# Causal attention: products and values moved around the score pairs of a step on TensorE

## The chip, the cores and the metric

The kernel runs on one NeuronCore of a Trainium2 chip. The engines that matter here are TensorE (PE; its weight loads are listed as PEld), VectorE (DVE) and ScalarE (ACT); each works through an instruction stream of its own, and semaphores tie them together. The metric is the time of one execution on the device in microseconds (us), the median of the runs.

## The reference, cut to what matters

A network of four layers, each with an attention and a feed-forward part, on 1024 tokens of 256 features, in float32. Two of its attentions are causal, with 16 heads of width 16, on one sequence of all 1024 tokens. The first is:

```python
_d['L0_attn_x'] = jax.random.normal(..., (1, 1024, 256), dtype=_x0.dtype)

def _L0_attn_ref(x, Wq, bq, Wk, bk, Wv, bv, Wo, bo):
    b, s, _ = x.shape                     # 1, 1024
    q = rope(proj(Wq, bq)); k = rope(proj(Wk, bk)); v = proj(Wv, bv)
    attn = jnp.einsum('bhqd,bhkd->bhqk', q, k) * scale
    causal = jnp.triu(jnp.ones((s, s), dtype=bool), k=1)
    attn = jnp.where(causal, -jnp.inf, attn)
    attn_weights = jax.nn.softmax(attn, axis=-1)
    out = jnp.einsum('bhqk,bhkd->bqhd', attn_weights, v)
    return jnp.einsum('bse,fe->bsf', out.transpose(0, 2, 1, 3).reshape(b, s, E), Wo) + bo
```

The other, in the feed-forward part of the second layer (`_attention` in `_L1_ffn_ref`), computes the same without rope and biases. Everything else of the network is untouched.

## The kernel before

The stages run one after another; `attend_causal` (L1114) is the body of both causal attentions, with the prefix a0h in the first and a2h in the second. It is cut into eight units: a unit is four heads (a quad Q) and one half of the queries (h, 512 of them), in the order (Q0,h0), (Q1,h0), (Q0,h1), (Q1,h1), then the same for Q2 and Q3.

The exponentials need the maximum of each row beforehand, so two kinds of work go on at once, some units apart:

- 48 **steps** g (4 of a unit with h=0, 8 with h=1), one for each block of 128 keys. A step has two **score pairs**, `scores(g, 0)` and `scores(g, 1)` (L1355), here S0 and S1: two heads each, keys by up to 512 queries, into three PSUM banks in turn. ScalarE takes four exponentials of them (L1455). **V**, `values(g - 1)` (L1377), multiplies the four results of the step in front with the values. 32 of the steps are diagonal: their scores get mask products (L1285) and are 512, 384, 256, 128 wide in turn.
- 48 **visits** x, one for each block of 128 queries and 512 keys. A visit, here A, has products in two pairs (L1313), each into one of two PSUM pairs, and VectorE takes the row maxima of them (L1481). For 32 of the visits, the diagonal ones, masks (L1285, eight products) come behind both pairs. Visit g+9 stands in step g from step 7 on; the first steps have two visits, and the last, 38, is that of visit 47. Steps 39 to 47 have none.

Single **events** on TensorE stand between them: **M** (L1338, the maxima of a unit turned into a row, which VectorE adds to the queries, L1497; steps 3, 7, 15, 19, 23, 31, 39), **P** (L1296 and L1297, eight times a quad's queries or keys put in place, which ScalarE copies, L1440 and L1442; steps 12, 13, 14 twice, 16, 17, 18 twice), **D** (L1388, the denominators of a unit, read by VectorE, L1504; steps 6, 10, 18, 26, 30, 34, 42 and one behind the last) and **R** (L1397, their reciprocals back, which VectorE multiplies with the unit's sums, L1512; steps 8, 12, 20, 28, 32, 36, 44 and one behind the last).

A's two pairs and all events share the two PSUM pairs in turn, `spare(key)`, by a count over all of them; `wait_spare` makes each wait until what lay there two uses before was read (`a_read`, `m_added`, `rounded`, `r_steps`, `on_done`). The first step of a unit waits for its M to be added (`m_added`). S0 of a step waits for the third exponential of the step in front, S1 for the first of its own, V for the last of the step in front (`p_ready`).

In a step of the loop at the end of TensorE's stream stand S0, A (with its masks; in step 39 M), S1, a second visit, M or P, V, then D and R. The order of all events on ScalarE and VectorE is fixed by the same table `after`.

Of the kernel before, what the change touches and what calls it, by code (L numbers as in the profile page):

```python
# [1113 lines left out]
def attend_causal(nc, core, name, qk, v, scale, masks_dram, before, sync, gpsimd):  # L1114
# [33 lines left out]
    for Q in range(2, QUADS):  # L1148
        x = min(x for x, vi in enumerate(visits) if UNITS[vi[0]][0] == Q)
# [19 lines left out]
    with ExitStack() as ctx:  # L1169
# [94 lines left out]
        def seg(x):  # L1264

            w, qb, s = visits[x]
            diag = s == UNITS[w][1]
            return qb, s, ((qb + 1) * P - s * HALF if diag else HALF), diag
# [12 lines left out]
        def _(pe):  # L1281
# [19 lines left out]
            def maxima(x):  # L1301

                w = visits[x][0]
                Q, h = UNITS[w]
                qb, s, n, diag = seg(x)
                if h == 0 and qb == 0:
                    pe.wait_ge(rounded, 4 * (Q + 1))
                for p in range(2):
                    wait_spare(pe, ("A", x, p))
                    ps = spare(("A", x, p))  # L1310
                    for u in range(2):
                        rows = slice(64 * u, 64 * u + K)
                        mm = pe.matmul(ps[:, u, 0:n], qt[rows, 2 * (Q % SLOTS) + p, qb * P:(qb + 1) * P],  # L1313
                                       kt[rows, 2 * (Q % SLOTS) + p, s * HALF:s * HALF + n], start=True, stop=not diag,
                                       tile_position=(64 * u, 0))
                    if not diag:
                        mm.then_inc(a_ready, 1)
                    elif x < 4:
                        mask_pair(x, p, n)
                if diag and x >= 4:  # L1320
                    for p in range(2):
                        mask_pair(x, p, n)

# [18 lines left out]
            def scores(g, p):  # L1342

                w, kb = steps[g]
                Q, h = UNITS[w]
                c0, n, diag = width(g)
                if kb == 0 and p == 0:
                    pe.wait_ge(m_added, w + 1)
                    pe.wait_ge(rounded, len(FIRST))
                if 4 * g + 2 * p >= 2:  # L1350
                    pe.wait_ge(p_ready, 4 * g + 2 * p - 1)
                for u in range(2):
                    t = 4 * g + 2 * p + u
                    rows = slice(64 * u, 64 * u + K)
                    mm = pe.matmul(core.bank[2 + t % 3][:, 0:n], kt[rows, 2 * (Q % SLOTS) + p, kb * P:(kb + 1) * P],  # L1355
                                   qt[rows, 2 * (Q % SLOTS) + p, h * HALF + c0:(h + 1) * HALF], start=True,
                                   stop=not diag, tile_position=(64 * u, 0))
                    if not diag:
                        mm.then_inc(s_ready, 1)
                if diag:  # L1360
                    for c in range(2):
                        for u in range(2):
                            t = 4 * g + 2 * p + u
                            mm = mask(pe, core.bank[2 + t % 3][:, 64 * c:64 * c + 64], 1, c, u)
                            if c == 1:
                                mm.then_inc(s_ready, 1)

            def values(g):

                w, kb = steps[g]  # L1370
                Q, h = UNITS[w]
                c0, n, diag = width(g)
                if kb == 0 and w:
                    pe.wait_ge(ou_done, w)
                pe.wait_ge(p_ready, 4 * g + 4)
                for b in range(4):
                    mm = pe.matmul(core.bank[5][32 * b:32 * b + 32, c0:HALF], v[:, kb, 4 * Q + b, :],  # L1377
                                   prob[:, (4 * g + b) % NP, 0:n], start=kb == 0, stop=kb == KEYS_OF[h] - 1,
                                   skip_group_check=True, tile_position=(0, 32 * b))
                mm.then_inc(av_done, 1)  # L1380
# [20 lines left out]
            def others(events):  # L1401
                for kind, x, *c in events:
                    if kind == "A":
                        maxima(x)
                    elif kind == "M":
                        max_rows(x)
                    elif kind == "D":
                        sums(x)
                    elif kind == "P":
                        place(x, c[0])  # L1410
                    else:
                        inverse(x)

            others(head)
            for g in range(len(steps) + 6):
                events = [e for e in after[g] if e[0] in "APM"]
                if g < len(steps):
                    scores(g, 0)
                    others(events[:1])
                    scores(g, 1)  # L1420
                    events = events[1:]
                others(events)
                if 0 < g <= len(steps):
                    values(g - 1)
                others([e for e in after[g] if e[0] in "DR"])

# [2120 lines left out]
```

## Time and profile before

| | us |
|---|---|
| median of 3 runs | 2784.68 (2775.67 to 2786.64) |
| the profiled execution | 2789.25 |
| its span | 2787.5 |
| first causal attention's steps (a0h), from the span's start | 68.4 to 249.9 |
| second one's (a2h) | 1469.9 to 1656.7 |

Of the span TensorE is busy for 2531.3 us, VectorE for 1627.8, ScalarE for 1259.5, GpSimd for 1289.6. In a timeline a row is one instruction or several alike that follow each other: start, length, engine, line of the code, operation, what it writes and reads, and in brackets how long the engine had been idle and what ended that. PEclk is the granted clock of TensorE as a share of full speed. A step's start is the start of its first L1355 row.

### The profile page before, as it was taken

What the parts mean: (1) busy time and instruction counts of PE and PEld (TensorE: products, weight loads), DVE (VectorE), ACT (ScalarE), POOL (GpSimd) and SP (SyncE); (2) the same over time, 40 slices, a digit from 0 to 9 for tenths busy, and PEclk for the clock granted to TensorE, in tenths of its full rate; (3) what the DMA queues carried; (4) which work ended last, traced back from release to release, by engine and by line L of the source; (5) the groups of instructions that cost most, each with busy time, mean ns of one, the idle gap of its engine ahead of it and who ended that gap; (6) DMA issues with size and microseconds to landing.
All of it is one profiled execution on the core that took longest, in us unless ns stands there. A gap on an engine that the chain in (4) does not pass through costs nothing. (4 is left out here: it accounts for less than half of the span.)

```text
span 2787.5 us, 40697 instructions
## 1 busy us (share of the span) xinstructions
PE 2531.3 (91%) x14471; PEld 1686.6 (61%) x14474; DVE 1627.8 (58%) x2168; ACT 1259.5 (45%) x2174; POOL 1289.6 (46%) x1130
## 2 busy tenths in 40 slices
PE   6887999878999999999878888789999989998798
PEld 4444777654444444444664446578888867776676
DVE  4663555577666766664436633477767745554555
ACT  4464333464555555555334552256555543333222
POOL 4100344486888888888521003254545523442243
PEclk9798999898999999999976979899999998998799
DMA  1000111121101101010000001100100001110111
GB/s 58 1 2 15 35 46 48 44 79 38 39 16 38 39 24 38 16 35 1 27 24 1 1 1 49 52 22 20 31 20 20 21 10 41 45 45 15 30 42 41
DMA packets 39709, 81.63 MB, mean 29 GB/s; under 512 B 7552, under 2 KB 21120, under 8 KB 39040
## 3 DMA queue, kind: packets, MB, share of 16 engines
q1 hardware_dynamic: 39264, 79.41, 10.2%
q8 instruction: 98, 1.61, 0.3%
q14 instruction: 59, 0.48, 0.1%
q10 hardware_dynamic: 288, 0.13, 0.0%
HBM read 59.07 MB, written 2.62 MB: 22 GB/s over the span
## 5 line engine op out<-in xcount | busy, mean ns | idle before, releaser
L2017 DVE TENSOR_REDUCE a1h_mseg<-bank 128x2 f32<-128x1024 f32 x256 | 302.7, 1222 | 187.3 <-PE bank L1774 173.4
L63 POOL TENSOR_TENSOR f_wh<-f_raw,ones_r 128x768 fp32r<-128x768 f32 (+1 forms) x74 | 111.8, 1511 | 545.6 <-PE bank L464 367.2
L1951 ACT ACTIVATE a1h_prob<-bank 128x512 f32<-128x512 f32 x366 | 206.1, 598 | 165.8 <-PE bank L1834 83.8
L1754 POOL TENSOR_TENSOR a_qk<-a_qk,a1h_prob 128x512 f32<-128x512 f32 x186 | 238.7, 1315 | 50.8 <-ACT a1h_prob L1951 50.8
L453 PE MATMUL bank<-x_norm_h,f_wh 128*128 128x512 f32 x592 | 244.2, 412 | 6.5 <-PEq L3247 2.5
L453 PE MATMUL bank<-x_norm_l,f_wh 128*128 128x512 f32 x592 | 238.7, 403 | 0.0
L453 PE MATMUL bank<-x_norm_h,f_wl 128*128 128x512 f32 x592 | 237.5, 401 | 0.0
L656 DVE SCALAR_TENSOR_TENSOR f_tf<-bank,f_bias,f_sg 128x512 f32<-128x512 f32 x148 | 111.0, 751 | 191.8 <-PE bank L453 185.4
L1832 PE MATMUL bank<-a1h_ql,a1h_k 128*128 128x512 f32 x512 | 203.2, 397 | 0.0
L544 ACT ACTIVATE f_hhi<-f_hf 128x512 fp32r<-128x512 f32 x124 | 78.3, 632 | 276.3 <-DVE f_hf L664 276.3
L1847 PE MATMUL bank<-a1h_prob,a_v 128*64 128x512 f32 x732 | 179.8, 604 | 0.0
L670 DVE TENSOR_TENSOR f_hlo<-f_hf,f_hhi 128x512 fp32r<-128x512 f32 x124 | 116.1, 938 | 82.7 <-ACT f_hhi L544 82.4
L533 ACT ACTIVATE f_sg<-bank,f_bias 128x512 f32<-128x512 f32 x148 | 101.9, 688 | 130.1 <-PE bank L453 130.1
L453 PEld LDWEIGHTS bank<-x_norm_h,f_wh 128*128 128x128 f32 x592 | 114.0, 192 | 50.8 <-issue 24.3
L453 PEld LDWEIGHTS bank<-x_norm_l,f_wh 128*128 128x128 f32 x592 | 114.1, 193 | 28.2
L364 POOL TENSOR_TENSOR f_wl<-f_raw,f_wh 128x768 fp32r<-128x768 f32 (+1 forms) x74 | 127.8, 1727 | 5.9
L453 PEld LDWEIGHTS bank<-x_norm_h,f_wl 128*128 128x128 f32 x592 | 114.7, 194 | 25.5
L464 PE MATMUL bank<-f_hhi,f_wh 128*128 128x512 f32 x296 | 118.5, 400 | 12.8 <-DVE f_hlo L670 12.8
L1831 PE MATMUL bank<-x_norm_h,a1h_kn 128*128 128x512 f32 x256 | 120.4, 470 | 4.7 <-DVE a1h_k L2012 3.4
L2871 POOL TENSOR_TENSOR l2a_rope<-l2a_rope,l2a_tab 128x512 f32<-128x512 f32 x64 | 81.2, 1276 | 88.9 <-ACT l2a_rope L2736 87.8
L1754 POOL TENSOR_TENSOR x_norm<-x_norm,a1h_prob 128x512 f32<-128x512 f32 x86 | 112.3, 1338 | 20.6 <-ACT a1h_prob L1951 20.6
L1455 ACT ACTIVATE a2h_prob<-bank 128x512 f32<-128x512 f32 (+3 forms) x192 | 83.7, 488 | 81.2 <-PE bank L1285 56.9
(595 smaller groups left out, 6337.8 us busy)
## 6 DMA issues: line engine op xcount, KB each, us to landing
f_raw<-in_l_w_dram SPq DMA_DIRECT2D x66, 385.0 KB, 3.1
a1h_st_q<-a_qk SPq DMA_DIRECT2D x128, 128.0 KB, 2.4
l2a_qkraw<-in_l2a_wqk_dram SPq DMA_DIRECT2D x32, 128.0 KB, 2.1
l2a_vraw<-in_l2a_wvg_dram SPq DMA_DIRECT2D x8, 512.0 KB, 3.8
f_raw<-in_l_w_dram SPq DMA_DIRECT2D x8, 449.0 KB, 3.3
a_qk<-l_keys SPq DMA_DIRECT2D x24, 128.0 KB, 2.8
a1p_raw<-in_l1a_w_dram SPq DMA_DIRECT2D x20, 128.0 KB, 2.1
a_qk<-in_l1a_wo_dram SPq DMA_DIRECT2D x16, 128.0 KB, 2.1
```

The lines of the kernel that those rows point to most:

```text
L63: return pool.tensor_tensor(dst, src, one.to_broadcast(list(src.shape)), ALU.mult)
L364: pool.tensor_tensor(wl[:, slot, :], raw[:, slot, 0:B], wh[:, slot, :].bitcast(F32), ALU.subtract).then_inc(w_split, 1)
L453: mm = pe.matmul(out[:, :], w[:, slot, c0:c0 + P], x, start=n == 0, stop=n == 3 * n_k - 1)
L464: mm = pe.matmul(acc[m][h][:, :], w[:, slot, c0:c0 + P], x[:, h, :], start=begin and n == 0, stop=False, skip_group_check=True)
L656: dve.scalar_tensor_tensor(tf[:, h, :], up[h][:, :], bias[:, slot, 1:2], sg[:, h, :], ALU.add, ALU.mult).then_inc(t_ready, 1)
L670: dve.tensor_tensor(hl[:, h, :], src[:, h, :], hh[:, h, :].bitcast(F32), ALU.subtract).then_inc(hl_ready, 1)
L1754: pool.tensor_tensor(out, first, slot_of[t % NP], ALU.add).then_inc(sum_done, 1)
L1831: pe.matmul(bank[:, :], kn[:, G % 2, a, keys], QA[n % 2][:, a, half(h)], start=True, stop=False)
L1832: mm = pe.matmul(bank[:, :], k1[:, a, keys], ql[:, n % 2, a, half(h)], start=False, stop=lo >= hi)
L1847: pe.matmul(core.bank[5][64 * a:64 * a + 64, :], v[:, kb, 2 * (n // 4) + a, :], slot_of[t % NP], start=kb == 0, stop=kb == TB - 1, skip_gr ...
L1951: act.activation(slot_of[t % NP], core.bank[2 + t % 3][:, :], ACT.Exp, scale=scale).then_inc(p_ready, 1)
L2017: dve.tensor_reduce(mseg[:, :, qb, s], spare(("A", n, k))[:, :, :], AX.X, ALU.max).then_inc(a_read, 1)
```

## The change

For a step with a visit TensorE's stream is now: both pairs of A, S0, the masks of A, V, S1, then a second visit with its masks, M or P, D and R. A step without a visit has S0, its M if there is one (step 39), V, S1, D and R. In the first step there is no V in front; that of the last step stands alone behind it. The head of the stage, and the streams of the other engines, are as before, and so is the turn in which A and the events use the two PSUM pairs.

```diff
--- before.py
+++ after.py
@@ -1317,7 +1317,11 @@
                         mm.then_inc(a_ready, 1)
                     elif x < 4:
                         mask_pair(x, p, n)
-                if diag and x >= 4:
+
+            def mask_maxima(x):
+
+                qb, s, n, diag = seg(x)
+                if diag:
                     for p in range(2):
                         mask_pair(x, p, n)
 
@@ -1402,6 +1406,8 @@
                 for kind, x, *c in events:
                     if kind == "A":
                         maxima(x)
+                        if x >= 4:
+                            mask_maxima(x)
                     elif kind == "M":
                         max_rows(x)
                     elif kind == "D":
@@ -1415,12 +1421,20 @@
             for g in range(len(steps) + 6):
                 events = [e for e in after[g] if e[0] in "APM"]
                 if g < len(steps):
+                    visit = events[0][1] if events and events[0][0] == "A" else None
+                    if visit is not None:
+                        maxima(visit)
                     scores(g, 0)
-                    others(events[:1])
+                    if visit is None:
+                        others(events[:1])
+                    else:
+                        mask_maxima(visit)
+                    if g:
+                        values(g - 1)
                     scores(g, 1)
                     events = events[1:]
                 others(events)
-                if 0 < g <= len(steps):
+                if g == len(steps):
                     values(g - 1)
                 others([e for e in after[g] if e[0] in "DR"])
```

TensorE in step 16, first attention, and at the start of step 17, before (names: put is the matrix that places a quad, P's products; prob the exponentials):

```order
L1355 MATMUL bank<-a0h_qt,a0h_kt 128x512 [waits a0h_p_ready]
L1355 MATMUL bank<-a0h_qt,a0h_kt 128x512
L1296 MATMUL bank<-x_norm_h,a0h_put 128x512 [waits a0h_lo1,a0h_a_read]
L1297 MATMUL bank<-x_norm_l,a0h_put 128x512
L1296 MATMUL bank<-x_norm_h,a0h_put 128x512
L1297 MATMUL bank<-x_norm_l,a0h_put 128x512
L1377 MATMUL bank<-a0h_prob,a_v 32x128 [waits a0h_p_ready]
L1377 MATMUL bank<-a0h_prob,a_v 32x128 x3
L1355 MATMUL bank<-a0h_qt,a0h_kt 128x512 [waits a0h_p_ready]
L1355 MATMUL bank<-a0h_qt,a0h_kt 128x512
L1313 MATMUL bank<-a0h_kt,a0h_qt 128x384 [waits a0h_a_read]
L1313 MATMUL bank<-a0h_kt,a0h_qt 128x384
```

And now, where L1359 and L1381 are the old L1355 and L1377:

```order
L1359 MATMUL bank<-a0h_qt,a0h_kt 128x512 [waits a0h_p_ready]
L1359 MATMUL bank<-a0h_qt,a0h_kt 128x512
L1296 MATMUL bank<-x_norm_h,a0h_put 128x512 [waits a0h_lo1,a0h_a_read]
L1297 MATMUL bank<-x_norm_l,a0h_put 128x512
L1296 MATMUL bank<-x_norm_h,a0h_put 128x512
L1297 MATMUL bank<-x_norm_l,a0h_put 128x512
L1313 MATMUL bank<-a0h_kt,a0h_qt 128x384 [waits a0h_a_read]
L1313 MATMUL bank<-a0h_kt,a0h_qt 128x384
L1313 MATMUL bank<-a0h_kt,a0h_qt 128x384 [waits a0h_rounded]
L1313 MATMUL bank<-a0h_kt,a0h_qt 128x384
L1359 MATMUL bank<-a0h_qt,a0h_kt 128x512 [waits a0h_p_ready]
L1359 MATMUL bank<-a0h_qt,a0h_kt 128x512
```

V (L1377) has left its place behind P and stands between S0 and S1 of its step; the next visit, whose second pair waits for ScalarE's copy of P (`rounded`), stands in front of the next S0 instead of behind it.

TensorE around R, from S1 of step 20 to S0 of step 21, before:

```order
L1355 MATMUL bank<-a0h_qt,a0h_kt 128x512 [waits a0h_p_ready]
L1355 MATMUL bank<-a0h_qt,a0h_kt 128x512
L1285 MATMUL bank<-a0h_mk 128x64 x4
L1377 MATMUL bank<-a0h_prob,a_v 32x512 [waits a0h_p_ready]
L1377 MATMUL bank<-a0h_prob,a_v 32x512 x3
L1397 MATMUL bank<-ident,a0h_rx 128x128 [waits a0h_rx,a0h_a_read]
L1397 MATMUL bank<-ident,a0h_rx 128x128 x3
L1355 MATMUL bank<-a0h_qt,a0h_kt 128x384 [waits a0h_p_ready]
```

And now (L1401 is the old L1397):

```order
L1359 MATMUL bank<-a0h_qt,a0h_kt 128x512 [waits a0h_p_ready]
L1359 MATMUL bank<-a0h_qt,a0h_kt 128x512
L1285 MATMUL bank<-a0h_mk 128x64 x4
L1401 MATMUL bank<-ident,a0h_rx 128x128 [waits a0h_rx,a0h_a_read]
L1401 MATMUL bank<-ident,a0h_rx 128x128 x3
L1313 MATMUL bank<-a0h_kt,a0h_qt 128x384 [waits a0h_a_read]
L1313 MATMUL bank<-a0h_kt,a0h_qt 128x384
L1313 MATMUL bank<-a0h_kt,a0h_qt 128x384 [waits a0h_on]
L1313 MATMUL bank<-a0h_kt,a0h_qt 128x384
L1359 MATMUL bank<-a0h_qt,a0h_kt 128x384 [waits a0h_p_ready]
```

R follows S1 directly, and the visit with its wait for VectorE's multiply (`on`) lies between R and the next S0.

## Rows read from the trace of the kernel before

**Rows 1.** Stretches of both attentions: length, busy us (instructions) by engine, PEclk, DMA.
```profile
core 0: us, PE busy (x) PEld busy (x) DVE busy (x) ACT busy (x) POOL busy (x), PEclk, DMA share, GB/s
68.40:249.90 181.50, 154.47 (x1376) 77.97 (x1376) 98.90 (x130) 100.50 (x216) 10.13 (x10) 0.83 0.00 1
1469.90:1656.70 186.80, 161.37 (x1376) 80.90 (x1376) 98.96 (x130) 100.81 (x217) 10.06 (x10) 0.78 0.00 1
```

**Rows 2.** Timeline, steps 34 to 36 at full clock: start, length, engine, instruction.
```profile
206.23 0.47 PE L1313 MATMUL bank<-a0h_kt,a0h_qt 64*128 64x256 f32 x4
206.49 1.09 ACT L1455 ACTIVATE a0h_prob<-bank 128x512 f32<-128x512 f32 x2 [0.34 <-PE bank L1355]
...
207.13 0.51 PE L1355 MATMUL bank<-a0h_qt,a0h_kt 64*128 64x512 f32 x2 [0.31 <-ACT a0h_prob L1455]
...
207.57 1.06 PE L1377 MATMUL bank<-a0h_prob,a_v 128*32 128x512 f32 x8
...
208.57 0.66 PE L1388 MATMUL bank<-ident,a0h_ou 128*128 128x128 f32 x4
...
209.15 0.50 PE L1355 MATMUL bank<-a0h_qt,a0h_kt 64*128 64x512 f32 x2
...
210.40 0.50 PE L1355 MATMUL bank<-a0h_qt,a0h_kt 64*128 64x512 f32 x2 [0.28 <-ACT a0h_prob L1455]
...
211.82 0.50 PE L1355 MATMUL bank<-a0h_qt,a0h_kt 64*128 64x512 f32 x2
```

**Rows 3.** Timeline, TensorE, steps 42 and 43, at the lower clock.
```profile
231.51 0.79 PE L1355 MATMUL bank<-a0h_qt,a0h_kt 64*128 64x512 f32 x2
...
233.05 0.80 PE L1355 MATMUL bank<-a0h_qt,a0h_kt 64*128 64x512 f32 x2 [0.75 <-ACT a0h_prob L1455]
...
233.77 1.93 PE L1377 MATMUL bank<-a0h_prob,a_v 128*32 128x512 f32 x8
...
235.64 1.12 PE L1388 MATMUL bank<-ident,a0h_ou 128*128 128x128 f32 x4
...
236.68 0.67 PE L1355 MATMUL bank<-a0h_qt,a0h_kt 64*128 64x512 f32 x2
```

**Rows 4.** Timeline, step 36 into 37: R and its reader.
```profile
214.63 0.66 PE L1397 MATMUL bank<-ident,a0h_rx 128*128 128x128 f32 x4
...
215.22 0.44 PE L1355 MATMUL bank<-a0h_qt,a0h_kt 64*128 64x384 f32 x2
215.32 0.69 DVE L1512 TENSOR_TENSOR a_on<-a0h_ou,bank 128x512 f32<-128x512 f32 x1 [0.56 <-PE bank L1397]
```

**Rows 5.** Timeline, step 30: a visit's masks and S1.
```profile
193.58 0.29 PE L1285 MATMUL bank<-a0h_mk 64*128 64x64 bf16 x8
...
193.71 0.36 PE L1355 MATMUL bank<-a0h_qt,a0h_kt 64*128 64x256 f32 x2
```

**Rows 6.** Timeline, P in step 13; then step 16 into 17.
```profile
131.41 0.51 PE L1296 MATMUL bank<-x_norm_h,a0h_put 128*128 128x512 f32 x1 [0.49 <-DVE a0h_mseg L1481]
...
132.54 1.06 PE L1377 MATMUL bank<-a0h_prob,a_v 128*32 128x512 f32 x8
...
145.90 1.02 ACT L1440 ACTIVATE a0h_qt<-bank 128x1024 fp32r<-128x1024 f32 x1
...
146.09 0.50 PE L1355 MATMUL bank<-a0h_qt,a0h_kt 64*128 64x512 f32 x2
...
146.98 0.44 PE L1313 MATMUL bank<-a0h_kt,a0h_qt 64*128 64x384 f32 x2 [0.21 <-ACT a0h_qt L1440]
```

**Rows 7.** Timeline, steps 19 and 20: M and its reader.
```profile
156.87 0.50 PE L1355 MATMUL bank<-a0h_qt,a0h_kt 64*128 64x512 f32 x2
...
158.55 1.11 PE L1338 MATMUL bank<-a0h_nident,a0h_mpos 128*128 128x128 f32 x8
...
159.70 1.22 DVE L1497 TENSOR_TENSOR a0h_qt<-a0h_qt,bank 128x1024 fp32r<-128x1024 f32 x1 [1.28 <-PE bank L1338]
...
160.59 0.50 PE L1355 MATMUL bank<-a0h_qt,a0h_kt 64*128 64x512 f32 x2
```

**Rows 8.** Stretches around the last M, columns as in rows 1.
```profile
218.00:224.00 6.00, 4.61 (x60) 2.68 (x58) 4.03 (x6) 2.21 (x8) 0.00 (x0) 0.95 0.00 0
224.00:230.00 6.00, 4.26 (x24) 1.55 (x24) 0.25 (x1) 3.90 (x8) 0.00 (x0) 0.50 0.01 3
```

## The prediction

> **What bounds the kernel now.** The change touches only `attend_causal`, which runs twice. I first took the table of stretches over both executions [rows 1]: 181.5 us and 186.8 us, 368.3 us of the span of 2787.5, so that a change of 0.5% of the kernel is 3.8% of these stretches. TensorE (PE) is listed busy for 154 and 161 us, VectorE for 99, ScalarE for 100: no engine is full, and PE's busy time contains its instructions' latencies. What sets the time is the order in which PE, which works its instructions off one behind the other, meets results of the other two. The mean granted clock is 0.83 and 0.78 there: between the two levels, 0.5 (1.2 GHz) and 1 (2.4 GHz), that is a third of the first stretch and 0.44 of the second at the lower one.
>
> Next the timeline, step by step. Of a step I write S0 and S1 for its two score pairs, V for the values of the step in front, A for a visit's products, D, R, M, P for the four kinds of single events. A plain step at full clock [rows 2]: S0 209.15, S1 210.40, next S0 211.82. S1 stands 1.25 us behind S0, because it waits for the first exponential of S0's scores; then S1 takes 0.44 (207.13 to 207.57) and V 1.00 (207.57 to 208.57), and 1.25+0.42+1.00 is the 2.67 us of the step. A lies in the hole between S0 and S1. D stands behind V and adds its 0.58 in full.
>
> **The steady step: no gain.** Now S0 is followed by V, which needs the last exponential of the step in front; that ends about one exponential (0.54, half of the pair at 206.49) behind the start of S0, so V starts almost at once. Then S1. The next S0 needs the third exponential, which hangs on S1 just as S1 hung on S0: 1.25 us behind S1. So 0.43+1.00+1.25 = 2.68 us, against 2.67. The hole of about 0.8 us has moved from behind S0 to behind S1, with A in it again. At half clock [rows 3] the same: before 1.54+0.72+1.87 = 4.13 (231.51, 233.05, 233.77, 235.64), now 0.72+1.87+1.54. The 48 steps of an attention thus give nothing by themselves. What counts is what else falls into which hole.
>
> **D and R where there is no visit (steps 42 and 44): gain.** They now lie behind S1, in an empty hole. At full clock all of D's or R's 0.58 goes; at half clock D takes 1.04 [rows 3], and 0.72+1.04 against 1.54 leaves 0.22 of it, a gain of 0.8. Together -1.4 us an attention. With a visit in the hole a D saves about 0.35 at full clock (0.43+0.58+0.47 for A = 1.48, where 1.25+0.58 stood), less the masks below; I get 0 for the D's there together, since in step 10 a copy on ScalarE, an extra one of that step, delays V.
>
> **R with a visit: loss.** A's two pairs take turns with the events in two PSUM pairs, so the second pair of the next A must wait until R's result was read. Before, that A stood behind the next S0 and the wait fell into the hole; now it stands in front of S0, and S0 waits with it. From R's start to the end of the multiply that reads it is 215.32+0.69-214.63 = 1.38 us [rows 4]. In step 36: S0 with its own four masks 0.50 (0.44, and half of the eight masks' 0.13 [rows 5]), A's masks 0.15, V 1.00, S1 0.50, then 1.38, 0.07 until PE starts, and the last pair 0.24 (half of 0.47 at 206.23): 3.84, against 3.40 (211.82 to 215.22). Five such steps (8, 20, 28, 32, 36) follow so, by between 0 and +0.8: +2.5.
>
> **P with a visit: loss.** P's reader is a 1.02 us copy on ScalarE, which stands behind all four exponentials of its step. In step 16 the copy runs 145.90 to 146.92, S0 of step 17 had started at 146.09, and A's second pair started at 146.98, waiting for the copy [rows 6]. Now S0 comes behind that pair: 146.98+0.24 = 147.22, +1.13 us, and ScalarE stands idle meanwhile. The other P steps lose little on balance: there P, 1.13 long (131.41 to 132.54), had itself waited for VectorE's first reduction (0.49 at 131.41), and with V in front of S1 this wait goes. All of steps 12 to 18: +1.5 (+0.14, +0.2, +0.2, step 16 +1.15, step 17 +0.1, step 18 -0.3).
>
> **M: both ways.** M's reader is the 1.22 us addition. For an M that nobody needed soon (step 19), M to the end of the addition is 159.70+1.22-158.55 = 2.37 [rows 7]; V used to fill it. Now 1.58 (S0, A's masks, V) +0.43 (S1) +2.37+0.07+0.24 = 4.69, against 3.72 (156.87 to 160.59): +0.97. Where S0 waited for the addition anyway (steps 7, 15, 31, 39), A standing earlier lets the reductions start earlier, worth about 0.4 in 31, in 39, and in steps 22 and 23 together; in 39, which has no visit and where M stays in front of V, the addition also runs beside V and S1, 0.4 more. The rest is near 0. Sum of M: -0.55.
>
> **Masks, and VectorE.** The masks of a diagonal visit cost PE 0.13 us (193.58 to 193.71 [rows 5]), and I take 0.15 in front of V. They lay in the hole behind S0 and now stand on the chain, and they let VectorE start its reduction only behind S0. With V narrow (steps 21 to 30) this shows. Following the remaining steps in this manner gives +1.1. Steps 0 to 7, where VectorE paces everything, end 0.1 us later: PE is blocked at the same reductions in both orders.
>
> **Sum.** -1.4 + 0 + 2.5 + 1.5 - 0.55 + 1.1 + 0.1 = +3.25 us an attention, +6.5 for two, all else unchanged. The profiled execution took 2789.25 us (1.75 around its span of 2787.5); so 2795.75 for it. It lay 4.6 above the median of the runs shown, 2784.68, so I forecast 2791.
>
> **What is not in the trace.** How long S0 really waits behind A in the new order is bounded: below by nothing (the reader is done in time, all holes used), above by a whole reader, about 1.2 us, on each of the 20 R, P and M events that have a visit behind them, 24 us an attention. I take my chains, since the readers' own rows are at hand. The masks in front of V, 0.13 at full clock, may cost twice that at half clock: 32 times 0.13, at most 4 us an attention; I take 0.15.
>
> **Rivals.**
> *Nothing changes* (2785): the plain step is symmetric, and the small losses and gains cancel. For it: terms of one sign are only a little larger. Chance 0.25.
> *Faster, events fill the holes.* It decides if a reader ends within the hole of 0.8 us, so that A never holds up S0. Then 26 events with a visit (12 D and R, 14 P and M) each save 0.35 and the last steps 1.4: 10.5 an attention, 2785-21 = 2764, and half of it where only the shorter readers fit, 2774. Against it: readers of 1.02 and 1.22 us, and 1.38 from R's start. Chance 0.12.
> *The clock.* [rows 8]: behind a thin stretch around an M the clock goes from 0.95 to 0.50, and at 231.51 a step still takes the long form [rows 3]. A step at half clock takes 4.13 instead of 2.67, so of each us spent there 0.35 is lost. The new order puts idle pieces of about 1 us in front of S0 in P and R steps, in a stretch that now has full clock. If 30 us more of each attention fell, it would cost 21: 2791+21 = 2812. Chance 0.15. The other direction, less half clock, belongs to the faster cases. The Trainium skill, "TensorE: Matmul & The Clock Gate", section "A second HAM failure mode: psum-queue depth-cycling", says that a kernel which micro-idles between matmul groups while cycling through PSUM banks sees its clock go back and forth between the levels. This trace agrees that it goes back and forth (0.95, 0.50 in neighbouring rows); by that rule the change, which adds such idles, would come out near this rival.
> *Reductions become the chain.* A diagonal visit's reduction starts 0.43 later behind S0, and if the next A waits for it in 17 of the 32 diagonal visits, 7 us an attention come on top: 2805. Against it: VectorE is busy for 99 of 181 us only. Chance 0.10.
> My forecast has 0.38, with a range of its own of 2782 to 2801.
>
> **Chances.** A difference of 0.5% (13.9 us) is about what can be told from no change. Slower by more than that (over 2798.6): 0.07 of the forecast, 0.13 of the clock, 0.08 of the reductions, 0.28. Faster (below 2770.8): 0.06 of the faster case, and 0.02 for more of the higher clock, 0.08. Within: 0.64. The range, 2774 to 2815, ends at the milder form of the faster case and just behind the clock's 2812.
>
> **What would show it.** Right: in the changed profile a plain full step of 2.7 us with V between S0 and S1; S0 directly behind a visit's second pair in R, P and M steps, that pair's wait put down to the multiply, the copy or the addition; D and R of steps 42 and 44 free; both attentions some 3 us longer at the same clock. Wrong: A's pairs without such waits (then faster), or a plain step other than 2.7 at full clock, or a mean clock in the two stretches off 0.83 and 0.78 by more than 0.05, which alone would outweigh the sum.

## The result and the profile after

| | us |
|---|---|
| before, median of 6 runs | 2783.47 (2775.67 to 2786.64) |
| after, median of 6 runs | 2801.4 (2795.41 to 2808.12) |
| ratio | 1.0066, 95% interval 1.0046 to 1.0086 |
| profiled execution of after, its span | 2799.14, 2797.4 |

The changed kernel is slower by 0.66%, 18 us. I had forecast 2791: the sign of the sum was right, its size was not, since +6.5 us had been the sum, about a third of what was measured. The profiled execution of before lay high (2789.25), so the two profiles differ by 10 us only.

Both attentions of after, in the view of [rows 1]:

```profile
core 0: us, PE busy (x) PEld busy (x) DVE busy (x) ACT busy (x) POOL busy (x), PEclk, DMA share, GB/s
68.30:258.10 189.80, 159.28 (x1374) 78.03 (x1374) 98.53 (x130) 100.75 (x216) 10.16 (x10) 0.81 0.00 1
1473.70:1664.20 190.50, 160.76 (x1374) 79.05 (x1374) 98.63 (x130) 100.75 (x216) 10.08 (x10) 0.80 0.00 1
```

They are 8.3 and 3.7 us longer, with nearly the same busy time on VectorE and ScalarE. The same view cut at S0 of step 10 and of step 39 shows where, in the first attention. Before:

```profile
68.42:118.27 49.85, 42.07 (x333) 22.90 (x334) 31.20 (x39) 19.04 (x45) 2.39 (x1) 0.62 0.00 1
118.27:220.12 101.85, 89.60 (x876) 46.13 (x873) 63.75 (x85) 64.86 (x134) 7.74 (x9) 0.95 0.01 1
220.12:248.50 28.38, 21.42 (x154) 8.33 (x150) 3.94 (x8) 16.04 (x37) 0.00 (x0) 0.76 0.00 1
```

And after:

```profile
68.35:118.15 49.80, 40.76 (x335) 21.34 (x335) 31.03 (x39) 18.59 (x44) 2.41 (x1) 0.66 0.00 1
118.15:226.88 108.73, 93.06 (x868) 46.99 (x869) 64.24 (x85) 65.26 (x135) 7.75 (x9) 0.92 0.01 1
226.88:256.75 29.87, 24.66 (x158) 9.21 (x158) 3.26 (x7) 16.41 (x37) 0.00 (x0) 0.66 0.00 1
```

Steps 0 to 9 are as long as before, though at a higher clock (0.66 against 0.62). The middle has grown by 6.9 us. The end, where the sum had its gain, is 1.5 us longer, at a clock of 0.66 against 0.76.

What PE waits for has changed owner. The view of waits on PE in the first attention, before (the instruction that waits, the one waited for; us in total, times, the longest):

```profile
PE bank L1355 <- ACT a0h_prob L1455: 9.9, 23, 0.7
PE bank L1313 <- DVE a0h_mseg L1481: 6.3, 11, 0.8
PE bank L1355 <- DVE a0h_qt L1497: 3.4, 5, 1.3
...
PE bank L1296 <- DVE a0h_mseg L1481: 2.3, 4, 1.0
...
PE bank L1313 <- ACT a0h_qt L1440: 0.2, 1, 0.2
```

And after:

```profile
PE bank L1359 <- ACT a0h_prob L1469: 7.8, 17, 0.9
PE bank L1313 <- DVE a0h_qt L1511: 6.5, 7, 1.1
PE bank L1313 <- DVE a0h_mseg L1495: 6.5, 11, 1.0
PE bank L1313 <- ACT a0h_kt L1456: 3.4, 4, 1.2
PE bank L1313 <- ACT a0h_qt L1454: 1.5, 2, 0.8
PE bank L1313 <- DVE a_on L1526: 1.1, 3, 0.4
```

The score pair waits 2.1 us less for exponentials. The visit's products waited 0.2 us for a reader of an event before. Now (L1313) they wait 12.5 us for those of M (`qt` on DVE, 6.5), P (`kt` and `qt` on ACT, 4.9) and R (`on`, 1.1), and mostly with S0 standing behind them. Not all of this is new: 3.4 us are the wait for M's addition that S0 itself had before (L1355 for `qt`) and has no more, and the 2.3 us that P's products (L1296) waited for reductions are gone too, as the prediction had it. All waits of this view together are 27.5 us before and 30.4 now.

The plain step of [rows 2] in the new order, step 35 at full clock:

```profile
215.66 0.40 PE L1359 MATMUL bank<-a0h_qt,a0h_kt 64*128 64x512 f32 x2
215.99 1.06 PE L1381 MATMUL bank<-a0h_prob,a_v 128*32 128x512 f32 x8
216.98 0.50 PE L1359 MATMUL bank<-a0h_qt,a0h_kt 64*128 64x512 f32 x2
217.32 0.34 PE L1313 MATMUL bank<-a0h_kt,a0h_qt 64*128 64x384 f32 x2
217.94 0.44 PE L1313 MATMUL bank<-a0h_kt,a0h_qt 64*128 64x384 f32 x2 [0.29 <-DVE a0h_mseg L1495]
218.23 0.50 PE L1359 MATMUL bank<-a0h_qt,a0h_kt 64*128 64x512 f32 x2
```

S0 to S0 is 2.57 us (2.68 forecast, 2.67 before): the step is symmetric but for 0.1, since V starts 0.33 behind S0.

Step 36, where R stands with a visit, answers to [rows 4]:

```profile
220.34 0.66 PE L1401 MATMUL bank<-ident,a0h_rx 128*128 128x128 f32 x4
...
221.04 0.69 DVE L1526 TENSOR_TENSOR a_on<-a0h_ou,bank 128x512 f32<-128x512 f32 x1 [0.29 <-PE bank L1401]
...
221.78 0.50 PE L1313 MATMUL bank<-a0h_kt,a0h_qt 64*128 64x512 f32 x2 [0.35 <-DVE a_on L1526]
...
222.12 0.34 PE L1359 MATMUL bank<-a0h_qt,a0h_kt 64*128 64x384 f32 x2
```

The second pair starts 1.44 us behind R's start, 0.05 behind the end of the multiply, and S0 follows 0.34 later. The step is 3.89 us long, where I had 3.84.

The same around P, from step 16 into 17, answers to the second part of [rows 6]:

```profile
148.27 1.02 ACT L1454 ACTIVATE a0h_qt<-bank 128x1024 fp32r<-128x1024 f32 x1 [0.89 <-PE bank L1297]
...
149.35 0.44 PE L1313 MATMUL bank<-a0h_kt,a0h_qt 64*128 64x384 f32 x2 [0.80 <-ACT a0h_qt L1454]
...
149.63 0.40 PE L1359 MATMUL bank<-a0h_qt,a0h_kt 64*128 64x512 f32 x2
```

ScalarE idles 0.89 us in front of its copy, PE waits 0.80 for it, and S0 of step 17 comes at 149.63: step 16 is 5.61 us long, against 3.15 before and 4.3 in my chain. The granted clock in that place (steps 15 to 17), and in one more (step 20), was 1.00 before and is now (rows of stretches, columns as above):

```profile
142.00:150.00 8.00, 6.39 (x44) 3.48 (x43) 2.51 (x3) 3.69 (x6) 0.00 (x0) 0.62 0.00 1
164.00:169.00 5.00, 4.61 (x36) 2.08 (x36) 1.79 (x4) 2.08 (x4) 0.00 (x0) 0.66 0.00 0
```

### The profile page after: what moved, and what is told of

Same layout as the page of the kernel before. It is cut to its first block and busy times, and to the rows that moved or that the text cites. A ratio compares the mean times of both kernels' runs of the same rounds, so it can differ in the third digit from the quotient of the medians.

```text
span 2797.4 us, 40700 instructions
## 1 busy us (share of the span) xinstructions
PE 2533.4 (91%) x14474; PEld 1683.6 (60%) x14474; DVE 1625.8 (58%) x2168; ACT 1260.3 (45%) x2174; POOL 1290.9 (46%) x1130
## 3 DMA queue, kind: packets, MB, share of 16 engines
HBM read 59.07 MB, written 2.62 MB: 22 GB/s over the span
## 5 line engine op out<-in xcount | busy, mean ns | idle before, releaser
L1469 ACT ACTIVATE a0h_prob<-bank 128x512 f32<-128x512 f32 (+3 forms) x192 | 83.8, 488 | 88.0 <-PE bank L1285 63.3
```

What stands on the lines that cost most here:

```text
L1469: act.activation(prob[:, t % NP, 0:n], core.bank[2 + t % 3][:, 0:n], ACT.Exp, scale=scale).then_inc(p_ready, 1)
```

## The experiments

Twelve more sets of runs stand here, of the changed kernel again and of eleven other orders, each beside the kernel before on the same chip; a ratio is to those runs beside it. The diffs are against the changed kernel's loop or the one named. For each run the mean granted clock of the whole execution is known too. Over the 98 runs of the kernel before in these sets, time falls by 1.87 us for each 0.001 of that clock (a straight line fitted to them; mean 2785.1 us at 0.9306; a single run scatters by 1.4 us around it). The last column is how far a kernel's mean lies above that line, called below its loss at equal clock. It is an account and not an experiment: no run held the clock. Lengths of steps at full clock, where PEclk is 1.00 over the step, are the second measure; they repeat within some 0.03 us from one execution to the next in most steps (step 19 of the changed kernel: 4.61 in all four attentions profiled).

| | ratio, 95% interval | clock | at equal clock, us |
|---|---|---|---|
| the change, first runs | 1.0066 (1.0046 to 1.0086) | 0.9272 | +9.9 |
| 1, the change again | 1.0064 (1.0046 to 1.0083) | 0.9275 | +9.7 |
| 2, V alone | 1.0034 (1.0016 to 1.0052) | 0.9313 | +8.8 |
| 3, products alone | 1.0139 (1.0120 to 1.0159) | 0.9224 | +25.3 |
| 4, last steps only | 0.9989 (0.9974 to 1.0003) | 0.9316 | -3.5 |
| 5, behind after M, P, R | 0.9988 (0.9975 to 1.0000) | 0.9331 | +1.8 |
| 6, masks in front | 1.0048 (1.0034 to 1.0062) | 0.9272 | +8.3 |
| 7, V by step | 0.9983 (0.9973 to 0.9993) | 0.9308 | -3.1 |
| 8, behind after R | 1.0013 (0.9997 to 1.0029) | 0.9326 | +8.4 |
| 9, behind after P | 1.0018 (1.0007 to 1.0029) | 0.9296 | +4.9 |
| 10, V by step, fewer | 0.9992 (0.9981 to 1.0003) | 0.9298 | -3.5 |
| 11, behind after P, R | 1.0013 (0.9999 to 1.0026) | 0.9318 | +5.2 |
| 12, behind after P, R, three M | 0.9985 (0.9972 to 0.9999) | 0.9343 | +2.8 |

**1. The changed kernel again**, no edit.

> The changed kernel once more, unaltered, for a second trace. Theory of the ring and the masks with new dips of the clock: the same losses at the same steps (16, 20, 22, 28, 36 of both attentions), each within 0.1 us where both traces have the same granted clock, and again dips to the lower clock inside steps 16 to 30, where the kernel before had none at steps 16 and 20; time 1.005 to 1.009 of before. Rival, dips by chance: the dips stand elsewhere or are gone in this trace and the attentions are each only 3 to 4 us longer than before.

Measured 2800.83 us. The loss repeats, and so do the steps: where both traces are at full clock they agree within about 0.1 us. Of steps 10 to 38 the falls of the clock repeat in one attention (steps 16, 20, 28 and 29) and stand elsewhere in the other.

**2. V alone.** V stands between the pairs, the visit with its masks behind S0 as before:

```diff
-                    visit = events[0][1] if events and events[0][0] == "A" else None
-                    if visit is not None:
-                        maxima(visit)
                     scores(g, 0)
-                    if visit is None:
-                        others(events[:1])
-                    else:
-                        mask_maxima(visit)
+                    others(events[:1])
                     if g:
                         values(g - 1)
                     scores(g, 1)
```

> Half of the change: V stands between the score pairs, the visit stays behind S0 with its masks. Theory of two holes: the hole behind S1 is now empty, so a plain full step costs 0.43+0.47+0.15+1.00+1.25 = 3.1 to 3.3 us instead of 2.67, some +15 us over 31 steps of an attention; but D, R, P fall into the empty hole (some -12), steps 42 and 44 save 1.4, and no reader's wait stands in front of S0. Near +2 us an attention, time 1.000 to 1.004 of before, and faster than the whole change by 10 us or more. Rival, the values' place itself is what costs: as slow as the whole change (1.006) or slower.

Measured 2796.03 us. The ratio is in the range, but it is only some 5 us (8 by the means) under the changed kernel, where I had expected 10 or more. A plain step takes 3.13 us (steps 11 and 35): A and V share the hole behind S0 and the one behind S1 stands empty. In compensation S0 waits for no reader of P or R (step 16: 4.70 against 5.61, both partly or wholly at the lower clock). Its clock, 0.9313, is no lower than before, though every plain step now has an empty hole.

**3. The products alone.** The visit stands in front of S0, V at the end of the step:

```diff
                     scores(g, 0)
...
-                    if g:
-                        values(g - 1)
                     scores(g, 1)
                     events = events[1:]
                 others(events)
-                if g == len(steps):
+                if 0 < g <= len(steps):
                     values(g - 1)
```

> The other half: the visit's products stand in front of S0, V stays at the end of the step behind M and P. Theory of two holes: the hole behind S0 holds only masks, V and A stand one behind the other on the chain, so a plain full step costs 1.25+0.43+1.00+0.47 = 3.15 us instead of 2.67, nothing is hidden for D, R, P, M: +15 us and more an attention, time 1.010 to 1.015 of before. Rival, the waits of the visit for the readers are the whole loss: those waits are partly covered by V here, so this is faster than the whole change (under 1.006).

Measured 2823.29 us, the worst. TensorE's rows of two steps at full clock:

```profile
232.49 0.40 PE L1359 MATMUL bank<-a0h_qt,a0h_kt 64*128 64x512 f32 x2
233.62 0.50 PE L1359 MATMUL bank<-a0h_qt,a0h_kt 64*128 64x512 f32 x2 [0.74 <-ACT a0h_prob L1467]
234.05 1.06 PE L1381 MATMUL bank<-a0h_prob,a_v 128*32 128x512 f32 x8
235.05 0.62 PE L1313 MATMUL bank<-a0h_kt,a0h_qt 64*128 64x384 f32 x4
235.50 0.39 PE L1359 MATMUL bank<-a0h_qt,a0h_kt 64*128 64x512 f32 x2
```

The hole behind S0 is empty (0.74 of waiting), and V and A both stand on the chain: 3.01 us. Its middle stretch, steps 10 to 38, ran at 0.80 in the first attention (0.87 in the second):

```profile
120.23:245.11 124.88, 105.22 (x870) 51.64 (x869) 64.27 (x85) 64.51 (x133) 7.51 (x9) 0.80 0.00 1
```

Runs 2 and 3 together are the test of the steady step: of the two holes one must hold V and the other A, and it makes little difference which (2.57 against 2.67 us). The rival of run 3, under 1.006, fell.

**4. Last steps only.** The order of before, with V between the pairs from step 40 on:

```diff
                 if g < len(steps):
                     scores(g, 0)
                     others(events[:1])
+                    if g >= 40:
+                        values(g - 1)
                     scores(g, 1)
...
-                if 0 < g <= len(steps):
+                if 0 < g < 40 or g == len(steps):
                     values(g - 1)
```

(against the kernel before)

> The new place of V in steps 40 to 47 alone, where there is no visit; steps 0 to 39 as before. Theory: D of step 42 and R of step 44 go into the hole behind S1, -0.8 and -0.6 us, two attentions -2.8 us, time 0.998 to 1.000 of before; the other six late steps unchanged to 0.1 us at the same clock. Rival: no gain there, since V delays S1; then 1.000 or above with late steps longer than before.

Measured 2780.03 us, and 3.5 us under the line at equal clock. The sum's term for these steps was 2.8 for both attentions. Not all of the other six late steps stayed within 0.1 us: step 41 took 4.38 us against 4.13 at the lower clock, and step 45 of the first attention 2.92 against 2.60.

**5. The visit behind S0 after M, P and R**, all else as in the change:

```diff
                     visit = events[0][1] if events and events[0][0] == "A" else None
-                    if visit is not None:
+                    shared = g > 0 and any(e[0] in "MPR" for e in after[g - 1])
+                    if visit is not None and not shared:
                         maxima(visit)
                     scores(g, 0)
                     if visit is None:
                         others(events[:1])
                     else:
+                        if shared:
+                            maxima(visit)
                         mask_maxima(visit)
```

> The whole change, except that a visit whose step follows one with an R, P or M stands behind S0 again (its second pair is the one that waits for the reader). Theory, the readers' waits in front of S0 are what the change loses: the waits of a visit's products for the copy, the multiply and the addition no longer hold S0 up, steps 16, 19, 20, 28 shorten by 0.5 to 1.4 us each at equal clock; but the following step then has S0, the visit, masks and V in one row and lengthens by 0.5 to 0.9, so that some 1 to 3 us an attention remain: 1.004 to 1.006 of before. Rival, the waits are the whole loss and nothing comes back: 1.000 to 1.002.

Measured 2782.22 us, ratio 0.9988. I had held that part of the gain is handed back, because A and V then share a hole (1.004 to 1.006); the rival, that the readers' waits are the whole loss (1.000 to 1.002), came nearer, and the result lies below both. Yet the steps do hand back: steps 36 and 37 take 2.93 and 3.62 us, 6.55 together, against 6.38 in the changed kernel and 5.99 before. Over steps 10 to 38 without 16, each at full clock, an attention is 1.5 us longer than before, where the changed kernel is 2.9 longer; so the steps did as I had held, and half of the chains' loss remains. Of the 18.7 us between the two kernels' means 8.0 are given back at equal clock, and 10.7 come with a clock of 0.9331 against 0.9273. In the first attention the middle stretch is at 0.95 again and the end at 0.86, where the changed kernel had 0.92 and 0.66 (in the second 0.97 against 0.94, and no difference at the end):

```profile
122.21:225.50 103.29, 89.94 (x870) 46.38 (x869) 64.45 (x85) 64.67 (x135) 7.74 (x9) 0.95 0.01 1
225.50:250.77 25.27, 19.75 (x160) 7.89 (x160) 3.25 (x7) 16.31 (x37) 0.00 (x0) 0.86 0.00 1
```

**6. Masks in front**, with the products:

```diff
                     if visit is not None:
                         maxima(visit)
+                        mask_maxima(visit)
                     scores(g, 0)
                     if visit is None:
                         others(events[:1])
-                    else:
-                        mask_maxima(visit)
```

> The whole change with the visit's masks in front of S0, directly behind its products, instead of between S0 and V. Theory: 0.15 us for each of some 24 diagonal visits leaves the chain, and VectorE's reductions of these visits start about 0.4 us earlier, which shortens steps 22, 27, 30 and 31, where the next visit waits for them: -4 to -5 us an attention, 1.002 to 1.004 of before. Rival, the masks cost nothing and VectorE is not the chain: as the whole change, 1.006.

Measured 2798.95 us, ratio 1.0048 against 1.0064 for run 1, each beside its own runs of before; the intervals overlap, and the ratio lies between my 1.002 to 1.004 and the rival's 1.006. The steps tell more: at full clock steps 22 and 30 are 0.4 and 0.5 us shorter than in the changed kernel, steps 23, 27 and 31 are 0.13 longer each, and the 25 steps of 10 to 38 that both show at full clock are 0.8 shorter together. So the masks' place is worth about 0.8 us an attention, and no large part of the loss hangs on it.

**7. V by step.** The order of before, with V between the pairs only where the steps' lengths in the first runs had it better (against the kernel before):

```diff
+                between = g in (8, 10, 12, 13, 17, 19, 23, 26, 28, 30, 34) or g >= 39
                 if g < len(steps):
                     scores(g, 0)
                     others(events[:1])
+                    if between:
+                        values(g - 1)
                     scores(g, 1)
...
-                if 0 < g <= len(steps):
+                if 0 < g < len(steps) and not between or g == len(steps):
                     values(g - 1)
```

> The order of before, visits behind S0 everywhere, and V between the score pairs only in steps 8, 10, 12, 13, 17, 19, 23, 26, 28, 30, 34 and from 39 on: where an event can lie in the hole behind S1, or where no visit stands in the hole behind S0. Theory of two holes, from the steps of the kernel with V moved alone: -0.8, -0.3, -0.7, -0.3, -0.3, -0.1, -1 or more, -0.4, -0.6, -0.2, -0.2 and -1.4 for the last steps, some -5 us an attention: 0.995 to 0.998 of before, the fastest of all. Rival, the gains of single steps are given back by the steps next to them or by the clock: 0.999 to 1.001.

Measured 2783.18 us, ratio 0.9983, with an interval just under 1. That lies between my range and the rival's. The rival's mechanism shows: what steps 13 and 17 gain, the steps behind them give back. At full clock step 13 went from 4.28 to 3.98 us and step 14 from 5.45 to 6.21 (second attention), step 17 from 4.58 to 3.95 and step 18 from 6.20 to 7.08 (first attention). Where the clock fell there as well, steps 14 and 18 took 7.51 and 8.48 us.

**8. Behind S0 after R alone**, and **9. after P alone**: run 5 with `"R"` or `"P"` in the place of `"MPR"`.

> The whole change, but the visit stands behind S0 again in the steps that follow an R (five an attention have a visit there), not in those behind an M or a P. With M, P and R alike treated so, the ratio to the kernel before was 0.9988; with none of them, 1.0064. By my terms R was 2.5 us an attention of a loss whose other reader terms are P's 1.5 and step 19's 0.97, so R alone should take back half of the 21 us: 1.002 to 1.004. Rival (the clock): the loss comes from a few stretches that fall to the lower clock anew, wherever an idle piece is the last straw; then one kind of reader taken away gives back either all (0.999 to 1.000) or next to nothing (1.006).

> As the run for R, but the visit stands behind S0 only in the steps that follow a P (12 to 19, all with a visit). If the three kinds of readers add up, this and the run for R should together give back about 0.0065 of the 0.0076, this one 0.002 to 0.004 of it: ratio 1.002 to 1.0045. Step 16, which measured 5.6 us where I had 4.3, should be back near 4.2 to 4.7, and steps 13 and 14 a few tenths shorter. Rival (the clock): ratio as in the other run at 0.999 to 1.000 or at 1.006, and the half-clock stretch that began at step 16 only moves to step 20.

Ratios 1.0013 and 1.0018: R gives back 0.0051 of the loss, P 0.0046, each more than half, together more than all of it. Both lie just under the ranges that I had given, and the interval of run 8 reaches the rival's 1.000. At equal clock R gives back only 1.4 us and P 4.9; R's gain came with a clock of 0.9326 against 0.9273, P's with 0.9296. The rival's second claim, all or nothing, holds for neither as measured. In run 9 step 16 took 4.11 us in the first attention, at the lower clock, and 2.70 in the second, at full clock, where the change had 5.61 and 5.33; I had expected 4.2 to 4.7.

**10. V by step, fewer**: run 7 without its steps 13 and 17.

> Order of before, with V between the score pairs in steps 8, 10, 12, 19, 23, 26, 28, 30, 34 and 39 to 47: the version of the previous job (ratio 0.9983) without its steps 13 and 17, where step 18 had become 0.9 to 2.3 us longer while step 13 gained less. If these two steps are to blame for that, 1 to 2 us an attention come back: 0.9970 to 0.9980. If step 18's length is only the clock's place in that execution, the ratio stays at 0.998 to 0.999.

Ratio 0.9992, where 0.9970 to 0.9980 was expected. Step 18 did go back to 6.20, and steps 13 to 18 of the first attention took 28.0 us against 29.6 in run 7, but the kernel as a whole is no faster: the clock was 0.9298 against 0.9308. Runs 7 and 10 can't be told apart: their intervals overlap, and at equal clock they differ by 0.4 us. Nor can either be told from run 4, which moves V in the last steps alone: -3.1, -3.5 and -3.5 us at equal clock. In the steps something is left: 10 to 38 without 32 and 33, each at full clock, are 1.4 us an attention shorter than before. That this reaches the kernel's time is not shown.

**11. Behind S0 after P and R**, and **12. after P, R and the M's of steps 15, 19 and 23**: in run 5 `"PR"` for `"MPR"`, and in run 12 also `g in (16, 20, 24)`.

> The whole change, with the visit behind S0 again in steps that follow a P or an R, not in those that follow an M alone. Kept from the change behind an M: the visit in front of S0 in steps 4, 8, 16, 20, 24 and 32. Two readings of what is on the chip so far. If the parts simply add (0.0051 taken back by R alone, 0.0046 by P alone, of 0.0064), this is 0.9967, and the visits behind an M gained 0.0021 when they stood in front, as the sign of my M term (-0.55 us an attention) had it. If the steps' lengths in the profiled runs decide, an M blocks as the others do: steps 19 and 20 together take 8.7 us in front against 7.7 behind, steps 22 to 24 9.5 against 8.9, 15 and 16 0.4 more, and only 7 and 31 gain (0.1 and 0.5): about 1.7 us an attention slower than with all three kinds behind (0.9988), so 1.000.

> As the last, and the visit behind S0 also in steps 16, 20 and 24, behind the M's of steps 15, 19 and 23; in front still in steps 4, 8 and 32. By the steps' lengths this is the best placing of the visits: 0.6 us an attention under the version with all three kinds behind, so 0.9984, with a bound of 0.998 to 0.9995. If the parts add instead, it lies above the run before it, which would be 0.9967: 0.998 or more here and less there.

Ratios 1.0013 and 0.9985. The parts do not add (that would have been 0.9967 for run 11, outside its interval); the steps' lengths, which gave 1.000 and 0.9984, come close. TensorE after M, from step 19 into 20, in the changed kernel (answers to [rows 7]):

```profile
161.96 1.11 PE L1342 MATMUL bank<-a0h_nident,a0h_mpos 128*128 128x128 f32 x8
163.00 0.39 PE L1313 MATMUL bank<-a0h_kt,a0h_qt 64*128 64x256 f32 x2
164.39 0.39 PE L1313 MATMUL bank<-a0h_kt,a0h_qt 64*128 64x256 f32 x2 [0.99 <-DVE a0h_qt L1511]
164.61 0.40 PE L1359 MATMUL bank<-a0h_qt,a0h_kt 64*128 64x512 f32 x2
```

And in run 12, where the lines of the products and the scores are the same and the addition is L1514:

```profile
161.27 0.50 PE L1359 MATMUL bank<-a0h_qt,a0h_kt 64*128 64x512 f32 x2
161.38 1.22 DVE L1514 TENSOR_TENSOR a0h_qt<-a0h_qt,bank 128x1024 fp32r<-128x1024 f32 x1 [1.76 <-PE bank L1342]
...
162.65 0.38 PE L1313 MATMUL bank<-a0h_kt,a0h_qt 64*128 64x256 f32 x2 [0.61 <-DVE a0h_qt L1514]
```

The addition is as late as before, but S0 is issued ahead of it. Run 12 is 0.8% under the change, and 0.15% under the kernel before (interval 0.01 to 0.28%), some 4 us; run 7 does as well, by 0.17%, with less of the change in it. The two are not alike: run 12 has the highest clock of all (0.9343) and lies 2.8 us above the line at equal clock, while run 7 lies 3.1 below it.

## Why the prediction was right in kind and short in size

**Steady step.** Right: 2.57 against a forecast of 2.68, symmetric, and runs 2 and 3 show what happens where both kinds of work share a hole.

**The chains at full clock.** Of steps 10 to 38 all but step 16 ran at full clock in some attention of both orders. I took those lengths from eight attentions: the two kernels' profiles, run 1's, and run 4's (which is the kernel before up to step 39).

| step | before | after | change | forecast |
|---|---|---|---|---|
| 12, 13, 14 | 4.85, 4.28, 5.45 | 5.01, 4.52, 5.57 | +0.16, +0.24, +0.12 | +0.14, +0.2, +0.2 |
| 17, 18 | 4.58, 6.20 | 4.68, 5.68 | +0.10, -0.52 | +0.1, -0.3 |
| 19 (M) | 3.71 | 4.61 | +0.90 | +0.97 |
| 20, 28, 32 (R) | 3.40, 3.59, 2.62 | 3.73, 3.50, 3.39 | +0.33, -0.09, +0.78 | 0 to +0.8 each |
| 36 (R) | 3.41 | 3.89 | +0.48 | +0.44 |
| 22 and 23 | 2.23, 4.43 | 3.23, 3.71 | +0.28 | -0.4 |
| 31 | 4.79 | 3.71 | -1.08 | -0.4 |
| 27 | 1.74 | 2.56 | +0.82 | in the +1.1 |

All 28 steps sum to +2.9 us; with my +1.15 for step 16, never seen at full clock in the new order, about +4.0. The terms that fall into this stretch had made +4.85 (R 2.0 without step 8, P 1.5, M +0.25 without step 39, the rest 1.1). So the readers' chains were right, mostly to 0.1 us where I had worked one out, and the stretch as a whole was 0.8 too dear (0.5 of it in R: 1.5 us where I had 2.0). The two misses, steps 22 and 23 and step 31, nearly cancel.

**The last steps.** Step 42 at the lower clock went from 5.17 to 4.35, -0.82, where I had -0.8; step 44 at full clock from 3.40 to 2.82, as forecast. These rows of after answer to [rows 3]:

```profile
237.91 0.79 PE L1359 MATMUL bank<-a0h_qt,a0h_kt 64*128 64x512 f32 x2 [0.75 <-ACT a0h_prob L1469]
238.63 1.93 PE L1381 MATMUL bank<-a0h_prob,a_v 128*32 128x512 f32 x8
240.50 0.79 PE L1359 MATMUL bank<-a0h_qt,a0h_kt 64*128 64x512 f32 x2
241.22 1.11 PE L1392 MATMUL bank<-ident,a0h_ou 128*128 128x128 f32 x4
242.26 0.79 PE L1359 MATMUL bank<-a0h_qt,a0h_kt 64*128 64x512 f32 x2
```

D lies in the hole behind S1. Step 39, with M ahead of V, went from 4.17 at full clock to 3.60 at 0.91, a gain of about 0.6 where I had 0.8, and two steps that I had left out lost a little: step 41 0.25 at the lower clock, step 45 0.3 in the first attention. But step 44 itself took 4.39 us in the profile of after, because the lower clock lasted until then: the gain was made and given back.

**What was mis-sized: "all else unchanged".** The sum was +6.5 us, 15.8 were measured as the difference of the means. The sum held the clock as it was in the one profiled execution. In steps 10 to 38 the changed kernel and its repeat took 108.7, 107.8, 107.7 and 110.4 us in their four attentions, mean 108.7; the kernel before and run 4 took 101.9, 103.4, 103.6 and 102.1, mean 102.8. That is +5.9 where the chains give +4.0 (with step 16's term). Part of step 16 or all of it was at the lower clock in all four attentions, and of steps 20, 28 and 29 in three of them; before, the falls lay in steps 23 to 26 and 31 to 33. A step that waits for a reader is longer by itself and longer once more at the lower clock: step 20 took 3.73 at full clock and 5.25 with two thirds of it at the lower one, steps 28 and 29 together 6.0 and 8.3.

By the line through the runs of before, 9.8 of the 15.8 us are there at equal clock, against my 6.5, and 6.0 come with a clock lower by 0.0032. The clock was my second rival, at 0.15 and priced at +21 with 30 us of each attention falling; it came at under a third of that price, together with the chains and not in their place. Both my forecast and this rival were thus partly right, which the chances had kept apart.

Of the other 3.3 us at equal clock a part lies at the start: from the first M to S0 of step 10 the changed kernel and run 1 take 53.1 us, the kernel before and run 4 51.7, with 37.5 us at the lower clock in both. That is +1.4 an attention, where the sum had about +0.6 (0.1, and step 8's part of R). With about +4.0 for the middle and, by the single steps above, -1.6 for steps 39 to 47 an attention loses 3.8, two lose 7.6. The other 2.2 us I can't assign: the line takes the clock's mean over the whole kernel, while an attention loses unlike amounts where its clock falls.

**What was luck.** The measured 2801.4 lies just past the forecast's own range (2782 to 2801); it is inside 2774 to 2815 because that range had been drawn out to the price of the clock's rival. The likeliest outcome I had named, within 0.5% of before, at 0.64, did not come; slower than that had 0.28.

**Idle pieces and the clock.** Taking the readers' waits out of S0's way (runs 5, 8, 9, 11, 12) went with a mean clock of 0.9296 to 0.9343 in place of 0.9273, and run 3, which waits in an empty hole in every step, has the lowest, 0.9224. Run 2 speaks against so simple a rule: it too leaves a hole empty in every plain step, the one behind S1, and its clock is 0.9313, above the 0.9306 of the kernel before. The Trainium skill, "TensorE: Matmul & The Clock Gate", section "A second HAM failure mode: psum-queue depth-cycling", says that micro-idles between matmul groups send the clock back and forth; all runs here but run 2 agree in direction. That these idles cause the falls is suggested, not shown: no run changed idle time and nothing else.

**Rivals.** *Nothing changes* fell by the interval. *Events fill the holes* fell: A's pairs do wait, 12.5 us in an attention. Yet its mechanism works where nothing shared follows, in steps 42 and 44, and run 4 is that piece by itself. *Reductions become the chain*: L1313 waits 6.5 us for reductions after and 6.3 before, and run 6, which lets the reductions start earlier, gains 0.16% (0.8 us an attention in the steps, for the most part in 22 and 30), not this rival's 7 us an attention; it fell.

## What to carry to other kernels

In an engine that works in order, an instruction moved ahead of the critical one brings all its waits with it: list who holds its buffer at that moment, and leave it behind where that holder is a long reader (here 1.0 to 1.4 us against a hole of 0.8). Of two equal holes neither is better, so judge such a move by the exceptional steps, step by step, and price them twice, once at the clock of the profile and once with the lower clock in the stretch that gets the new idle time. The same moves that cost 18 us when made everywhere gained about 4 in the best versions by step (runs 7 and 12). Only the move in the last steps, where nothing stands in the hole, is shown to gain at equal clock (run 4, 3.5 us, though the interval of its ratio still holds 1); run 7 has no more than that, and run 12's gain comes with the clock.

## What the runs showed of the hardware

- The place where TensorE's clock falls differs between executions of one kernel, and between attentions with the same order of work: the changed kernel fell in steps 15, 16, 20, 28 and 29 in one attention, its repeat in 15 to 17, 24, 25, 32 and 33 in another. A single profile is one draw from this; the profiled execution of before had 143 us of its two attentions at the lower clock, run 4 only 118, with the same order up to step 39.
- A mean clock higher by 0.001 went with 1.87 us less in 98 runs of the kernel before. Their times spread over 25.7 us (2774.42 to 2800.11), and a run scatters by only 1.4 us around the line, so most of the spread goes with the clock.
- The parts of this loss did not add: R's waits removed gave 0.0051, P's 0.0046, both 0.0051. The clock took part in it (0.9326, 0.9296 and 0.9318 against 0.9273).
